# Two fused transformer layers on one core: second norms one third of a tile ahead, the last group stored by blocks, 32 products with the identity turned into transposes

## The reference

```
h = layernorm(x) * (1 + ca) + sa
x = x + ga * L0_attn(h)        # gated delta-rule recurrence, state 64x64, y normalised by RMS, then @ Wo.T
h = layernorm(x) * (1 + cb) + sb
x = x + gb * L0_ffn(h)         # ternary weights: silu(gate) * up (2048 wide), RMS norm, project to 512
h = layernorm(x) * (1 + ca) + sa
x = x + ga * L1_attn(h)        # wkv scan over time with running maximum, k, v, r from time-mixed h, then @ Wo.T
h = layernorm(x) * (1 + cb) + sb
x = x + gb * L1_ffn(h)         # weights as integer codes: silu(gate) * up (1408 wide), project to 512
```

## Time and profile before

| | |
|---|---|
| median of 3 executions | 1212.82 us (1211.11 to 1213.15) |
| profiled execution | 1210.19 us |
| its span, first to last instruction | 1208.1 us |
| mean granted TensorE clock | 0.930 of full speed |
| TensorE matmul busy | 1083.9 us (90%) |
| VectorE busy | 872.7 us (72%) |
| ScalarE busy | 526.0 us |
| GpSimd busy | 169.3 us |

### The profile page before, as it was taken

One profiled execution on the slowest core, in us unless ns is written; L12 is line 12 of the kernel. 1 busy time (PEld: TensorE's weight loads), 2 busy tenths in 40 slices (PEclk: granted clock), 3 DMA queues, 4 the chain that ended last, 5 costly groups with the idle time before them and its releaser, 6 DMA issues. The chain is left out here.

```text
span 1208.1 us, 13011 instructions
## 1 busy us (share of the span) xinstructions
PE 1083.9 (90%) x4345; PEld 525.2 (43%) x4392; DVE 872.7 (72%) x1606; ACT 526.0 (44%) x1100; POOL 169.3 (14%) x143
## 2 busy tenths in 40 slices
PE   6788877689997989898889899999998999999997
PEld 3446633444443444344344354444444444444443
DVE  4887765556665778987779799488897587785654
ACT  4656644235443455435255354154435163531421
POOL 3101000011111322122122122122202000100100
PEclk9857867579999999999999999999999999999999
DMA  8411111413220133323220002013020011020000
GB/s 268 175 53 53 36 36 18 174 41 100 88 87 1 48 126 102 89 64 117 66 84 27 27 27 96 2 44 101 27 69 9 1 53 36 18 70 1 1 35 35
DMA packets 47523, 75.55 MB, mean 63 GB/s; under 512 B 8320, under 2 KB 16000, under 8 KB 47328
## 3 DMA queue, kind: packets, MB, share of 16 engines
q1 hardware_dynamic: 47168, 74.62, 19.6%
q0 software_dynamic: 288, 0.09, 0.2%
HBM read 66.16 MB, written 8.54 MB: 62 GB/s over the span
## 5 line engine op out<-in xcount | busy, mean ns | idle before, releaser
L1491 PE MATMUL g_g<-h,wt 128*128 128x512 f16 x1728 | 402.9, 382 | 5.9 <-DVE hid L1793 2.4
L1491 PEld LDWEIGHTS g_g<-h,wt 128*128 128x128 bf16 (+1 forms) x1728 | 168.5, 99 | 224.6 <-issue 37.1
L1505 PE MATMUL g_d<-wt,parts 128*128 128x512 bf16 (+1 forms) x831 | 200.1, 381 | 7.6 <-DVE tmp L1624 2.7
L2113 ACT ACTIVATE parts<-hid 128x512 f16<-128x512 f32 x108 | 68.2, 631 | 306.9 <-DVE hid L1793 306.9
L1414 PE MATMUL g_o<-shared 128*128 128x512 f32 x384 | 178.5, 608 | 13.6 <-DVE tmp L1585 5.6
L1786 DVE SCALAR_TENSOR_TENSOR hid<-th,g_g 128x512 f32<-128x512 f32 x108 | 73.6, 681 | 125.7 <-ACT th L2106 125.5
L1505 PEld LDWEIGHTS g_d<-wt,parts 128*128 128x128 f16 x864 | 83.8, 99 | 113.5 <-issue 15.7
L2223 POOL TENSOR_TENSOR acc<-acc,sqh 128x512 f32<-128x512 f32 x52 | 76.7, 1475 | 312.9 <-ACT sqh L2119 312.9
L1414 PEld LDWEIGHTS g_o<-shared 128*128 128x128 f32 x384 | 73.2, 194 | 95.1 <-issue 70.1
L1798 DVE TENSOR_TENSOR parts<-hid,parts 128x512 f16<-128x512 f32 x108 | 89.8, 832 | 26.8 <-ACT parts L2113 26.6
L2206 POOL TENSOR_TENSOR g_rstd<-g_var,g_power 128x4 f32<-128x4 f32 x20 | 24.2, 1212 | 328.9 <-DVE g_var L1531 328.9
(11 more groups left out here) (319 smaller groups left out, 1527.7 us busy)
## 6 DMA issues: line engine op xcount, KB each, us to landing
shared<-in_w SPq DMA_DIRECT2D x48, 256.0 KB, 2.7
x<-in_codes SPq DMA_DIRECT2D x32, 264.0 KB, 3.1
w_raw<-in_wt SPq DMA_DIRECT2D x16, 512.0 KB, 3.7
x<-in_wmod SPq DMA_DIRECT2D x7, 1024.0 KB, 5.2
wmod<-in_wmod SPq DMA_DIRECT2D x5, 1024.0 KB, 10.2
codes_f<-x SPq DMA_DIRECT2D x32, 132.0 KB, 1.7
gates<-in_x SPq DMA_DIRECT2D x4, 1024.0 KB, 8.0
x<-in_x SPq DMA_DIRECT2D x4, 1024.0 KB, 6.2
```

Source lines behind the costliest of these rows:

```text
L1491: mm = nc.tensor.matmul(pg[i][:], wide[:, k, o:o + P], h16[f % 2][:, s, k], start=(s == 0 and k == 0), stop=(s == 1 and k == KD - 1))
L1505: mm = nc.tensor.matmul(pd[j][:], parts16[:, t % 3, s, j * P:(j + 1) * P], wd[:, m, :], start=(m == 0 and s == 0), stop=(done and s == 1))
L2113: nc.scalar.activation(parts16[:, t % 3, 0], hid[:, t % 2], ACT.Copy).then_inc(hi_ready, 1)
```

## The change

There are four edits. In the head, the product with the identity at line 590 becomes a transpose, as its three neighbours are. In `y_transposes` the same is done for four products of each group. The second attentions' norms are put one step q earlier: statistics at a = -2 and -1, root at q = ATT[i] - 1, rows and `edge` at a = 1; the transposes on TensorE and the copies on ScalarE stay at a = 4 to 7. And the last group is stored in four transfers of 256 KB, each waiting for its own block's add, instead of one of 1024 KB.

```diff
@@ transposes(u, j)
-            nc.tensor.matmul(dst[:, 0:P], kt[u % 2][:, j, 0], ident[:], start=True, stop=True)
+            nc.tensor.transpose(dst[:, 0:P], kt[u % 2][:, j, 0], ident[:])
             nc.tensor.transpose(dst[:, P:2 * P], kt[u % 2][:, j, 1], ident[:])
@@ y_transposes(i)
             for j in range(NJ):
-                t = nc.tensor.matmul(dst[0:NS, j * P:(j + 1) * P], yn[:, j], ident[:], start=True, stop=True)
+                t = nc.tensor.transpose(dst[0:NS, j * P:(j + 1) * P], yn[:, j], ident[:])
             t.then_inc(full, 1)
@@ vector_program, residual
                 add_to(xs[f % NG], j)
+                block_no[f, j] = adds.n
             add_no[f] = adds.n
@@ vector_program, side
                 a = q - ATT[i]
-                if -1 <= a < 1:
-                    norm_stats(i, 2 * (a + 1))
-                    norm_stats(i, 2 * (a + 1) + 1)
-                    if a == 0:
+                if -2 <= a < 0:
+                    norm_stats(i, 2 * (a + 2))
+                    norm_stats(i, 2 * (a + 2) + 1)
+                    if a == -1:
                         norm_sums(("y", i))
-                if a == 2:
+                if a == 1:
                     norm_rows(("y", i))
                     edge(i)
@@ pool_program, side
-                if q == ATT[i]:
+                if q == ATT[i] - 1:
                     root("y", i)
@@ sync_program
+        def store_block(i, j):
+            g = ORDER[i]
+            sp.wait_ge(added, block_no[NG + i, j])
+            sp.dma_start(dram["out"][g * TG + j * P:g * TG + (j + 1) * P, :], xs[i][:, j]).then_inc(out_done, 16)
...
-            store_x(NG - 1)
-            sp.wait_ge(out_done, NG * 16)
+            for j in range(NJ):
+                store_block(NG - 1, j)
+            sp.wait_ge(out_done, (NG - 1 + NJ) * 16)
```

More of the change, by code:

```diff
@@ L1286, in freed @@
         return side_free[use[key] % 2]
-    root_no, var_no, add_no, code_no, roots = {}, {}, {}, {}, []
+    root_no, var_no, add_no, block_no, code_no, roots = {}, {}, {}, {}, {}, []
     c, adds = Count(None, steps), Count(None, added)
```

## The result

| | before | after |
|---|---|---|
| median | 1213.15 us (1211.11 to 1216.47) | 1203.53 us (1200.58 to 1206.69) |
| ratio of the times | | 0.991, 95% interval 0.9892 to 0.9928 |
| span of the profiled execution | 1208.1 us | 1201.5 us |

The change makes the kernel 9.6 us faster; 13.3 us were forecast, 1199.5 against 1203.5 us. The time lies inside the range of 1194 to 1207.5, and just outside the 1196 to 1203 that the forecast gave itself.

What follows compares the result with a forecast made beforehand. TensorE, busy 90% of the span, was taken to bound the kernel from about 264 us on. Norms 7.1, y transposes 2.4, head 1.7 and store 2.1 sum to 13.3 us: 1212.8 to 1199.5 us, range 1194 to 1207.5.

Steps and rivals of the forecast that it cites:

- Norms: Second attentions' norms one step earlier: most of TensorE's 7.58 us wait for rows at four sites goes; gain 7.1 us.
- ATT 54: First moved norm: rows ready in time, but the third piece needs ScalarE's evacuation, giving back some 0.7; gain 1.9 us.
- ATT 110: Second moved norm: 2.02 of rows and 0.80 of gate, less 0.4 for the up product; gain 2.4 us.
- the sum then starts up to 3 us later ... so it costs nothing: GpSimd's sum of squares behind the root at two moved norms: ScalarE needs it only two tiles on, cost nothing.
- y transposes: Four matmuls fewer at four places: 0.9 us at the first, 0.49 at three inside saturated tiles; gain 2.4 us.
- Head: 16 products become transposes; in six places VectorE next waits for TensorE's queue; gain 1.7 us, bounds 0 and 5.2.
- Store: Last group stored by blocks: the last store lands 2.4 us after issue instead of 4.5; gain 2.1 us.
- Reference: Gain subtracted from the runs' median 1212.8 us; the profiled execution was 2.6 us under it.
- longer stretches between the sites: Sign in the profile after: prediction wrong if the expected local signs hold but stretches between the sites are longer.
- Rival (a): VectorE's scans or ScalarE's evacuations take back most of the norms' gains, head gains nothing: 1206 us, chance 0.2.
- Rival (b): Less head work keeps the clock at 0.5 from 104 to 216 us: 23 us more, 1223 us, chance 0.06.
- Rival (c): A transpose saves nothing, as the operand wait sets the pace: 4.1 us missing, 1203.6 us, chance 0.04.

Runs made afterwards that it cites:

- the second ratio: The changed kernel timed and profiled once more, nothing else altered: 1203.38 us, ratio 0.9905 to the kernel before.
- second profile: The kernel before, unchanged, timed and profiled again: 1215.55 us, ratio 1.0009, profiled span 1213.5 us against 1208.1 in its first profile.
- sum_after_rows: The changed kernel with GpSimd's sum of squares of tiles 18, 36 and 55 waiting for the normalised rows: 1200.2 us, ratio 0.9887 to the kernel before.
- transposes_only: The kernel before with only the products with the identity, 16 in the head and 16 for y, made transposes: 1206.62 us, ratio 0.9937.

## Why the prediction was right, and where not

The sign and the range held; the forecast was 4.0 us too low, and the gain 9.6 to 11 us (11.5 by the second ratio) for 13.3. Its sum was 7.1 + 2.4 + 1.7 + 2.1 = 13.3; the parts give about 4.8 + 2.7 + 3.7 + 2.1 = 13.3 again, by other numbers. That the sum is the same is luck: 3.5 of it (2.0 in the head, 1.5 at tile 12) are losses by the clock that the profile which I forecast from doesn't have, and the combination seems to lose some 2 to 3 of it.

- **Norms, 7.1 forecast, 4.8 measured.** Step by step: ATT 54 1.35 for 1.9, ATT 110 1.4 for 2.4, ATT 166 1.2 for 2.2, ATT 222 0.8 for 0.6. The mechanism was right (waits for the rows at the four sites 1.5 for 7.58, gate product 0.93 late, up projection of ATT 110 at its time). The step that failed is "the sum then starts up to 3 us later ... so it costs nothing": I weighed GpSimd's sum by who waits for its result, and not by what it does to VectorE beside it, 0.96 + 0.26 + 1.10 (the last at ATT 166, where the kernel before had it too). The second miss is ScalarE's evacuation behind the code conversions: at ATT 54 I had 0.7 given back and 0.92 was waited, at ATT 110 I had none of it and it was 0.60.
- **y transposes, 2.4 forecast, 2.7 measured, for other reasons.** Four matmuls took 1.06 instead of 1.97 us at the first place, 0.9 as forecast, but before tile 0 0.2 to 0.5 of that was gone again: there the kernels with products gain 0.52 to 0.58 on the first profile, those with transposes 0.09 to 0.30. At tile 11 it was 0.7 for 0.49. At tiles 27 and 43 it was nothing: the place is no saturated tile, TensorE waits there for VectorE, from 3.01 to 3.15 and from 2.59 to 3.28. The clock at tile 12 gave 1.5 against the four profiles that lose there, nothing against the first.
- **Head, 1.7 forecast, 1.7 to 2.0 fixed and 2.0 by the clock.** Six places were counted and five or six found. The 2.0 are against four of five profiles with products.
- **Store, 2.1 forecast, 2.2 in the profile and 2.1 timed.**
- **Reference.** I subtracted the sum from the median of the runs, and took care that the profile was 2.6 us under it, but not that its places are one draw: no loss at tile 28, between 147 and 184 us and at tile 12 (2.7, 2.0 and 1.4 in the second profile), 3.4 too much at tiles 1 and 2. The prediction's own sign of being wrong, longer stretches between the sites, is there at tiles 28 and 44, and for tile 28 the reason is in good part this reference: the kernel before's second profile lost 2.67 there too.
- **Together.** At tile 28 after lost 2.92, where the parts that hold y's products lost 1.7 (once 2.67), and at tile 44 it lost 1.60, where only kernels with the norms moved lose anything. 13.3 less 1.2 and 1.6 leaves 10.5, and measured were 9.6 and 11; this sum was made behind the result and proves nothing. Both losses are by the clock (6.63 at tile 27; 5.31 + 5.40 at tile 43, 5.40 + 3.70 in the first profile; 3.70 is eight at full clock). Both profiles of after have them and sum_after_rows has 1.7 and 1.3; why the combination loses more than its parts is not shown.

Rival (a) is partly what happened, in mechanism: the evacuations took back some, VectorE's scans nothing (between tiles 45 and 55 no offset grew by over 0.02). Rival (b) named a place where the clock does move the time, but nothing was lost there: from 147 to 184 us after takes as long as the first profile and 2 us less than the second. The Trainium skill's rule (TensorE: Matmul & The Clock Gate, Part 4: PE-mode transpose) that the full clock's release doesn't engage for transposes would have had the head slower with 16 more of them; no kernel here shows that, and between 147 and 184 us the nine with them are 2 us faster than four of the five profiles without. Rival (c) gave 1203.6 us, which is what was measured, by coincidence: it is out by the rows at 57 us and by transposes_only, 7.7 us faster.

## What to carry to other kernels

When a step is moved in time, look at what the other engines do during its new place, and at each pair of VectorE and GpSimd instructions that come to lie beside each other, and not only at who waits for whose result. A wait that ends opens the one behind it: follow the next engine's queue, here ScalarE's, with everything in it. And profile the kernel before twice before a forecast in which 3 us matter, since steps of 1.5 to 3 us came and went with the clock from one execution to the next.

## What was unexpected of the hardware

- VectorE's operation on 4 columns took 1.24 us instead of 0.16 beside a GpSimd sum, and four rows took 2.87 instead of 1.92; with the sum behind them, 0.15 and 1.92.
- Sixteen transposes in place of products didn't lower the granted clock between 147 and 184 us: it is 0.72 to 0.73 in nine of nine kernels with them, and 0.69 to 0.70, with 2.0 us more, in four of five profiles with products. At tile 12 it is likewise: no loss in nine of nine with y's transposes, 1.4 to 1.5 us in four of five with products.
- A product with the identity is two matmul records, and a transpose is one: 0.61 against 0.22 us at half clock, and 1.09 for eight against 0.60 for four at full clock.
- After waits of 1.6 to 3.3 us TensorE's next eight matmuls took from 3.70 to 6.63 us, in no order by the wait's length; after 3.01 us one kernel took 3.70 in one execution and 6.37 in another.
